# Eight places instead of four for the rounded products of the third feed-forward pass

## The reference, cut to what matters

```python
def act_qdq(x):                       # one scale for the whole tensor
    scale = max(max(abs(x)) / 32767, 1e-12)
    return clip(round(x / scale), -32768, 32767) * scale
x = act_qdq(x)
up = act_qdq(x @ lpbq_dequant(w_up).T)          # 768 features
gate = act_qdq(x @ lpbq_dequant(w_gate).T)
sig = fixed_qdq_u16(sigmoid(gate))
gate = act_qdq(gate * sig)
o = act_qdq(gate * up)
return o @ lpbq_dequant(w_down).T               # back to 256
```

## Time and profile before

| | |
|---|---|
| median of 3 runs | 598.54 us (598.26 to 599.53) |
| the profiled execution | 599.63 us, span 597.6 us |
| mean granted TensorE clock | 0.951 |
| TensorE busy in 549.5 to 597.6 us (third pass and end) | 39.70 us of 48.10 |
| VectorE, ScalarE busy there | 34.67 and 30.98 us |

### The profile page before, as it was taken

One profiled execution on the slowest core, in us unless ns is written; L12 is line 12 of the kernel. 1 busy time (PEld: TensorE's weight loads), 2 busy tenths in 40 slices (PEclk: granted clock), 3 DMA queues, 4 the chain that ended last, 5 costly groups with the idle time before them and its releaser, 6 DMA issues. The chain is left out here.

```text
span 597.6 us, 10965 instructions
## 1 busy us (share of the span) xinstructions
PE 524.0 (88%) x3921; PEld 456.4 (76%) x3921; DVE 410.5 (69%) x1077; ACT 298.4 (50%) x858; POOL 123.6 (21%) x137
## 2 busy tenths in 40 slices
PE   2999999999999999999999999997639999500997
PEld 2988889888988988888898898885528888400996
DVE  4779744754764574575476458658748989999685
ACT  3635532632542362363254335327325569897773
POOL 3001301220221130122022112213031029900000
PEclk9999999999999999999999999999959999855799
DMA  7922001101100110110110001005001000100033
GB/s 257 361 88 72 1 1 54 37 1 54 35 0 0 53 35 0 53 35 0 35 45 8 1 2 36 2 1 160 0 19 35 2 0 1 35 1 1 1 106 105
DMA packets 18478, 25.86 MB, mean 43 GB/s; under 512 B 1216, under 2 KB 15808, under 8 KB 18448
## 3 DMA queue, kind: packets, MB, share of 16 engines
q1 hardware_dynamic: 18192, 25.17, 12.8%
q0 software_dynamic: 256, 0.30, 0.2%
HBM read 21.27 MB, written 4.19 MB: 43 GB/s over the span
## 5 line engine op out<-in xcount | busy, mean ns | idle before, releaser
L804 ACT ACTIVATE probs<-bank,nmax 128x129 f32<-128x129 f32 x256 | 90.9, 368 | 117.8 <-DVE nmax L1132 117.7
L1551 POOL TENSOR_TENSOR probs<-probs,rinv 128x512 f32<-128x512 f32 x64 | 66.7, 1042 | 337.8 <-DVE rinv L1140 337.8
L607 PE MATMUL bank<-wv,ctxT 128*128 128x512 f32 x384 | 94.2, 397 | 0.0
L599 PE MATMUL bank<-ctxT,wk 128*128 128x256 f32 x672 | 88.9, 282 | 0.0
L599 PEld LDWEIGHTS bank<-ctxT,wk 128*128 128x128 f32 x672 | 83.6, 188 | 0.0
L607 PEld LDWEIGHTS bank<-wv,ctxT 128*128 128x128 f32 x384 | 70.5, 188 | 16.9 <-issue 1.2
L1144 DVE COPY pT<-bank 128x512 f32<-128x512 f32 x64 | 43.7, 682 | 20.7 <-PE bank L670 18.7
L599 PE MATMUL bank<-xnT,wq 128*128 128x256 f32 x336 | 54.7, 298 | 0.0
L785 ACT ACTIVATE oT<-bank 128x256 fp32r<-128x256 f32 x64 | 24.7, 386 | 60.0 <-PE bank L679 60.0
L804 ACT ACTIVATION_READ_ACCUMULATOR probs<-bank,nmax 128x1 f32 x256 | 52.0, 203 | 0.0
L599 PEld LDWEIGHTS bank<-xnT,wq 128*128 128x128 f32 x336 | 43.2, 188 | 7.2 <-issue 1.2
(11 more groups left out here) (170 smaller groups left out, 810.6 us busy)
## 6 DMA issues: line engine op xcount, KB each, us to landing
craw<-in_ctx SPq DMA_DIRECT2D x8, 512.0 KB, 3.3
stage<-in_L_xattn_Wkv SPq DMA_DIRECT2D x8, 512.0 KB, 11.9
xa<-in_x SPq DMA_DIRECT2D x8, 256.0 KB, 2.7
xr<-in_x SPq DMA_DIRECT2D x8, 256.0 KB, 2.8
x_scratch<-y SPq DMA_DIRECT2D x7, 256.0 KB, 2.1
x2all<-x_scratch SPq DMA_DIRECT2D x1, 1792.0 KB, 8.3
xres<-x_scratch SPq DMA_DIRECT2D x6, 256.0 KB, 2.8
out<-yout SPq DMA_DIRECT2D x6, 256.0 KB, 2.2
```

The source lines that it names most:

```text
L599: last = mm(bk[:, n * TG:(n + 1) * TG], wt[a][:, k, f], act_t[b][:, k, :], start=(k == 0 and i == 0), stop=(k == kk - 1 and i == len(TERMS ...
L607: last = mm(bk[:, :], ctxT[a][:, k, b * S:(b + 1) * S], wv[w][:, k, h * 512:(h + 1) * 512], start=(k == 0 and i == 0), stop=(k == KC - 1 a ...
L804: last = nc.scalar.activation(probs[:, c % 2, u, 0:NK], score_bank[c % 2][h][:, b * QW:b * QW + NK], ACT.Exp, bias=nmax[:, c % 2, u:u + 1] ...
L1551: G.tensor_tensor(probs[:, c % 2, :, 0:S], probs[:, c % 2, :, 0:S], rinv[:, c % 2, :].rearrange("p (u o) -> p u o", o=1).to_broadcast([P, ...
```

## The change

A constant `OR = 8` is the number of places. `oint(n)` now lies in `tpi`, whose four chunks of 1024 columns make eight halves of 512; piece n has half n mod 8. Both waits ask for the low part of piece n-8 in place of n-4 (`ol_ready` at n-7). `tui` keeps the `ui` pieces in its first two chunks. Nothing else is changed; no instruction of an engine is added, removed or moved, but for the waits whose count becomes zero or less, which are not issued.

```diff
         GS = 6
+        OR = 8
...
         def oint(n):
-            return tui[:, 2 + n % 4 // 2, n % 2 * HC:(n % 2 + 1) * HC]
+            return tpi[:, n % OR // 2, n % 2 * HC:(n % 2 + 1) * HC]
...
             def prepare(n):
                 if rounded_by_scalar(n):
-                    wait(act, ol_ready, n - 3)
+                    wait(act, ol_ready, n - OR + 1)
...
             def o_integers(n):
                 if rounded_by_scalar(n):
                     return
-                wait(dve, ol_ready, n - 3)
+                wait(dve, ol_ready, n - OR + 1)
```

## The result

| | before | after |
|---|---|---|
| median of 11 runs | 599.81 us (598.26 to 601.25) | 594.95 us (593.42 to 597.47) |
| the profiled execution | 599.63 us, span 597.6 | 595.47 us, span 593.4 |
| last transpose of the scales (L719 or L720) starts at | 549.75 | 549.20 |
| first matmul of the third pass | 553.87 | 553.31 |
| last matmul ends | 594.85 | 590.68 |

The ratio is 0.992, interval 0.9905 to 0.9936, that is 3.8 to 5.7 us. Of the 4.2 us between the two spans 3.62 lie in the third pass (45.10 less 41.48). The other 0.55 us was there when the pass began, in code that is the same in both kernels.

A forecast was written before the change was run, and what follows sets the result against it. A ScalarE-VectorE round trip was taken to starve TensorE; with TensorE as the new bound, its matmuls end at 591.1 against 594.86, and 3.7 us off the 598.54 median gives 594.8 us, range 593.5 to 596.8.

The forecast's parts named there:

- What bounds: Third pass: serial high part, low part, rounding between ScalarE and VectorE; pieces come every 1.67 us, TensorE needs 1.43.
- The address at nothing: Rounded products move from `tui` to `tpi` in the third pass; the new address was costed at nothing.
- The waits: Third pass: VectorE's wait at L1490 ends nothing today; ScalarE's at L962, 7.6 us ahead of L963, goes.
- The loads of the three engines: Third pass, six pieces: ScalarE 7.5 us, VectorE 8.1, TensorE 8.6, all below today's 10.03; TensorE becomes the bound.
- The sum: Third pass: 27 slow matmuls to 559.64, then 261 at 0.119; last ends 591.1 against 594.86, 3.7 us less.
- What else could stop it: Third pass: last low part ready near 584 to 585, wanted at 586.7; output pair after piece 21 waits until near 581.7.
- The clock: TensorE's start in the third pass: a clock rise 1 us earlier or later moves the end by 0.44 us.
- its three terms: Upper end of the range: later clock 0.4 us, second handshake 1.1, and 0.7 by which three runs of before stray.
- rival 1: Third pass: ScalarE's high parts wait for VectorE's product L1497; only 2.6 us less, 595.9; chance 0.12.
- rival 2: Third pass: something unseen keeps the six-piece period at 10.03 us; no change within 0.2%, 598.5; chance 0.06.
- rival 3: Third pass: overlapping engines slow each other in SBUF; slower once VectorE's 8.1 us grow beyond some 23%; chance 0.04.

The follow-up runs named there:

- e4: Changed kernel with ScalarE alone waiting at n-3 as before; 45.10 us from last scale transpose to last matmul's end, ratio 0.999.
- e1: Kernel before with its four places moved into `tpi`, waits unchanged; 45.10 us from last scale transpose to last matmul's end, ratio 0.9982.
- e6: Kernel before with 42 added matmuls warming TensorE ahead of the third pass; 45.11 us from last scale transpose to last matmul's end, ratio 0.9987.
- e8: Kernel before without the third matmul of each three, output incomplete; 43.64 us from last scale transpose to last matmul's end, ratio 0.9988.
- e3: Changed kernel with VectorE alone waiting at n-3 as before; 40.85 us from last scale transpose to last matmul's end, ratio 0.9908.
- e2: Changed kernel with five places instead of eight, waits at n-4; 41.57 us from last scale transpose to last matmul's end, ratio 0.9916.
- e5: Changed kernel with 42 added matmuls warming TensorE ahead of the third pass; 39.24 us from last scale transpose to last matmul's end, ratio 0.990.
- e7: Changed kernel without the third matmul of each three, output incomplete; 36.18 us from last scale transpose to last matmul's end, ratio 0.9852.
- e9: Changed kernel with VectorE making each of 12 even products twice; 43.47 us from last scale transpose to last matmul's end, ratio 0.9981.
- e10: Changed kernel with VectorE making each of its 8 gate factors twice; 41.27 us from last scale transpose to last matmul's end, ratio 0.9949.

## Why the prediction was right

**What bounds.** That ScalarE and VectorE held each other up by a serial step, and TensorE starved from it, is shown by e4 and e1 (the wait and nothing else brings 45.10 back) and by e6 and e8 (neither a faster nor a relieved TensorE moves the kernel before, beyond its last block).

**The address at nothing.** Right, by e1. The mean of L1498 is 747 ns after, 745 before.

**The waits.** Right that VectorE's ended nothing (e3) and ScalarE's all. What the prediction didn't ask is how many places are needed; five do (e2).

**The loads of the three engines.** VectorE's 8.1 us for six pieces was measured at 8.13, TensorE's spacing of 0.119 us was 0.120 after ((12.00 + 0.283)/102, with 102 matmuls in 12 us). ScalarE takes 7.42 us from one L969 to the next (559.85 to 567.27), the forecast was 7.5. That TensorE is the bound after the change is shown by e5 and e7.

**The sum.** Forecast 3.7 us less for the pass; measured 3.62, at nearly the same rise of the clock (5.77 and 5.85 us). The matmuls took 37.37 us where the sum had 591.1 - 553.87 = 37.2.

**What else could stop it.** The last low part was to be there by 584 to 585, with some 2 us in hand; it was there at 583.44, with 2.7. The output pair after piece 21 was to wait until about 581.7; it waited, and started at 581.37, in a pass that began 0.56 us earlier. One thing was missed: VectorE's waits for high parts didn't shrink to the very first pieces; one of 0.93 us at 561.72 is left, where ScalarE also makes a gate factor (L969). It lies on no path.

**The clock.** The forecast of 0.44 us for each microsecond of rise was measured at 0.44. Its weight in the forecast was too small. The medians differ by 4.86 us, the forecast had 3.7. The profile of before had a rise of 5.77 us, and I took that for the changed kernel as it stood. In the eight cold profiles with the same pause ahead of the pass (all but e9 and e10, where it is 0.8 us longer) the rise came after 4.38 to 6.04 us, which makes the gain of the pass 3.5 (e2, 41.57) to 4.25 us (e3, 40.85). As the kernel before is blind to the rise and the kernel after is not, every rise sooner than the profiled one adds to the gain. At the mean of the eight, 5.20 us, the gain is 3.9 (an estimate: 3.62 and 0.65 times 0.44). So this term, which the forecast mis-sized, is worth some 0.3 us of the 1.2 between 3.7 and 4.86. The other 0.9 or so no run places; the interval, 3.8 to 5.7, reaches down to 3.9.

**The number, and luck in it.** That 594.8 was said and 594.95 measured is partly luck. The 3.7 was taken from 598.54, the median of three runs of before; eleven give 599.81, and 599.81 - 3.7 is 596.1. The low start (1.27 us) and the gain that was larger than forecast (1.16 us) cancel almost to nothing. What the runs bear out is the 3.62 of the pass. The range has a slip too: 594.8 and its three terms, 0.4, 1.1 and 0.7, make 597.0 and not 596.8, and the three runs of before stray by 0.99 to one side and 0.28 to the other, not by 0.7.

**The rivals.** The second handshake (rival 1) exists in one wait of 0.71 us at 579.2, behind which there was slack; with 1.98 us more of products for six pieces it becomes the bound (e9). That nothing would come of it (rival 2) needed a cause that isn't there. That overlap slows the engines in SBUF (rival 3) didn't occur: the low part's median is 688 ns, before it was 692. Its threshold was said to be 23% of VectorE's 8.1 us, 1.9 us for six pieces, for the time of before to return. With 1.98 added 43.47 us were measured, not 45.10. The price was set too high because the 8.1 us hold the two output pairs (1.58 us), which the first quarter doesn't have. In e9 VectorE takes 8.38 us from the low part of piece 2 to that of piece 8 (555.81 to 564.19) and 9.94 to that of piece 14 (574.13); in the kernel before the first of these two distances was 10.02 (556.87 to 566.89). The 1.64 us between 8.38 and 10.02 are the difference of the stretches, 1.63.

## What to carry to other kernels

Where two engines wait for each other in turn and neither is full, look for a buffer place that is written again too soon. Here the wait that closed the circle was on ScalarE, the engine that runs ahead, and one place more was enough. Add up each engine's work for one period: the gain ends at the largest of the sums, not at the idle time in the list. Once an engine with a cold start becomes the bound, its start counts (2.24 us here), where it had counted for nothing before. And a whole run can stray by more than the change is worth, while the stretch between two marks inside the trace repeats; compare that.

## What the runs showed of the hardware

In the eight cold profiles in which TensorE had done the same and rested as long, its granted clock rose between 4.38 and 6.04 us after the first matmul of the third pass; the moment differs from one execution to the next. In e9 and e10, which reach that matmul 0.8 us later, it rose after 3.85 and 3.54 us. The Trainium skill, "TensorE: Matmul & The Clock Gate", section "What's actually happening", says that the count of matmuls before the rise varies between runs of one kernel. These profiles agree with it, as far as kernels that differ only behind the start of the pass can stand for one kernel.

The slow matmuls stand 0.214 us apart (27 in 5.77 us), the fast ones 0.119 to 0.120 (103 starts in 12.28 us before, 102 after), which is not half: a change to the full clock saves 0.094 to 0.095 us for each. The same page, section "Wait — 56ns, not 53.3ns?", gives N / 1.2 GHz at the lower clock, which makes 0.213 us for 256 columns (an estimate by the page's formula), and the trace agrees with that. At the full clock its N / 2.4 GHz and 2.5 ns make an estimate of 0.109 us, and the trace lies above it.

I hadn't expected that the point ahead of the pass would lie up to 4.6 us apart (547.31 to 551.88) from profile to profile, while the pass itself repeats to 0.01 us where the moment of the rise doesn't enter (45.10 and 45.11, and 39.24 twice). TensorE's timelines of the 13 profiles show where the difference arises. The first part is there when the attention's output projections begin that lie halfway (L643 or L644), at 242.66 to 245.28 us; from them to the last transposes of `fraw` it is 179.2 to 179.6 us in all 13. The second lies between these transposes (L629 or L630, near 423 us) and the first transpose of the scales, near 438: 15.0 us in nine profiles, 17.1 to 17.2 in e3, e5, e6 and e10. In e3 the clock stood at 0.50 from 423 to 429 us, where before's stood at 1.00, and the same 24 matmuls took half as long again:

```profile
425.47 2.97 PE L648 MATMUL bank<-wout,oT 128*128 128x256 f32 x24
```

```profile
426.05 4.51 PE L649 MATMUL bank<-wout,oT 128*128 128x256 f32 x24
```

The third is the moment of the rise in the first matmuls for `gate`, from which it is 39.6 to 41.1 us to the second transpose of the scales: their first 12 took 5.49 us in before, after, e2 and e4, which needed 40.9 to 41.1, and 4.36 to 4.76 us in the other nine, which needed 39.6 to 40.0. From there to the last transpose all 13 take 64.08 to 64.12 us. So two of the three parts go with TensorE's clock; what makes the first one, ahead of 244 us, is open, and no run was made for any of them.
